# Scan stage of a two-layer decoder: late gate activations split in two, residual passes and two gate products moved

## The reference, cut to what matters

```python
xn = x * rsqrt(mean(x * x) + EPS) * norm_w
x_inner, z = split(xn @ in_proj_w.T, 2)          # 512 channels each
xc = silu(conv(x_inner) + conv_b)
x_ssm = xc @ x_proj_w.T                          # B (16), C (16), dt (1)
dt = softplus(x_ssm[..., -1:] * dt_w + dt_b)
A = -exp(A_log)
def step(h, inp):                                # over the 128 tokens
    dA = exp(dt_t[..., None] * A)
    h = dA * h + (dt_t * u_t)[..., None] * B_t[:, None, :]
    y_t = sum(h * C_t[:, None, :], axis=-1) + D_param * u_t
    return h, y_t
y = scan(step) * silu(z)
out = y @ out_proj_w.T + residual
```

## Time and profile before

| what | value |
|---|---|
| runs | 852.97, 853.94, 859.43 us |
| median | 853.94 us |
| profiled execution: its own time | 856.85 us |
| its span in the trace | 854.6 us |
| mean granted TensorE clock (share of full speed) | 0.923 |
| PE busy | 694.7 us (81%) |
| DVE busy | 673.3 us (79%) |
| ACT busy | 529.8 us (62%) |
| POOL busy | 497.3 us (58%) |
| first scan starts, last scan starts | 575.9, 732.3 us |

### The profile page before, as it was taken

One profiled execution on the slowest core, in us unless ns is written; L12 is line 12 of the kernel. 1 busy time (PEld: TensorE's weight loads), 2 busy tenths in 40 slices (PEclk: granted clock), 3 DMA queues, 4 the chain that ended last, 5 costly groups with the idle time before them and its releaser, 6 DMA issues. The chain is left out here.

```text
span 854.6 us, 22547 instructions
## 1 busy us (share of the span) xinstructions
PE 694.7 (81%) x8285; PEld 522.1 (61%) x8285; DVE 673.3 (79%) x1498; ACT 529.8 (62%) x1439; POOL 497.3 (58%) x528
## 2 busy tenths in 40 slices
PE   4899999999999989369999708988889988851464
PEld 3578888888888776158899503345555555441333
DVE  6767778898888976667788557789889998679867
ACT  2644555566555655236676595579899787019296
POOL 2057777777777875045555176118899898424211
PEclk9999999999999999669999858999999999975778
DMA  7827000000000410027775533032333332010001
GB/s 295 279 94 301 1 2 2 7 1 8 1 8 8 161 51 14 7 69 217 225 201 147 120 115 89 2 100 78 102 101 127 103 108 96 3 49 0 1 13 38
DMA packets 30347, 71.44 MB, mean 84 GB/s; under 512 B 5472, under 2 KB 19488, under 8 KB 28320
## 3 DMA queue, kind: packets, MB, share of 16 engines
q1 hardware_dynamic: 25680, 57.54, 19.3%
q0 software_dynamic: 4560, 12.46, 6.1%
HBM read 59.57 MB, written 10.42 MB: 82 GB/s over the span
## 5 line engine op out<-in xcount | busy, mean ns | idle before, releaser
L1911 POOL TENSOR_TENSOR arena<-arena 128x1024 f32<-128x1024 f32 x63 | 147.2, 2385 | 29.1 <-DVE arena L1850 23.5
L1850 DVE TENSOR_TENSOR_SCAN arena<-arena,ps 128x1024 f32<-128x1024 f32 x64 | 141.8, 2270 | 14.1 <-ACT arena L1720 6.9
L1537 PEld LDWEIGHTS ps<-arena 64*64 64x64 f32 x4096 | 79.6, 134 | 63.9 <-DVE arena L1850 25.5
L1537 PE MATMUL ps<-arena 64*64 64x64 f32 x4096 | 92.0, 223 | 17.9 <-issue 8.9
L647 PE MATMUL ps<-arena 128*128 128x128 f32 (+1 forms) x768 | 101.2, 282 | 0.9 <-PEq L376 0.9
L647 PEld LDWEIGHTS ps<-arena 128*128 128x128 f32 (+1 forms) x768 | 91.7, 193 | 14.1 <-issue 12.9
L852 ACT ACTIVATE arena<-arena 128x128 f32<-128x128 f32 x256 | 98.8, 390 | 1.2 <-DVE arena L776 1.1
L1088 POOL DMA_INDIRECT arena<-tokens,arena x63 | 60.8, 965 | 59.6 <-PE ps L1124 42.4
L860 ACT ACTIVATE arena<-ps 128x512 f32<-128x512 f32 x64 | 38.2, 597 | 86.6 <-PE ps L666 86.6
L907 POOL TENSOR_TENSOR arena<-arena 128x512 f32<-128x512 f32 x64 | 66.7, 1043 | 21.5 <-DVE arena L782 21.5
L897 POOL TENSOR_TENSOR arena<-arena 128x256 f32<-128x256 f32 x64 | 47.9, 748 | 46.2 <-DVE arena L762 46.2
(11 more groups left out here) (326 smaller groups left out, 1522.1 us busy)
## 6 DMA issues: line engine op xcount, KB each, us to landing
arena<-c_rows SPq DMA_DIRECT2D x32, 512.0 KB, 3.7
arena<-in_E_gu SPq DMA_DIRECT2D x8, 1024.0 KB, 12.9
expert_out<-arena SPq DMA_DIRECT2D x63, 128.0 KB
arena<-in_E_dn SPq DMA_DIRECT2D x1, 4096.0 KB, 13.3
arena<-in_ctxT SPq DMA_DIRECT2D x2, 1024.0 KB, 5.1
arena<-in_A_o SPq DMA_DIRECT2D x1, 2048.0 KB, 16.6
arena<-in_X_o SPq DMA_DIRECT2D x1, 2048.0 KB, 23.7
arena<-in_F_w SPq DMA_DIRECT2D x4, 512.0 KB, 5.2
```

The source lines that it names most:

```text
L1537: t = eng.matmul(psD[d][cols, k, at:at + R], dtuT[rows, b, c, cols], diagB[rows, i % 2, b, :], start=True, stop=True)
L1850: eng.tensor_tensor_scan(hst[s % 4], dA[s % 4], psD[s % 2].rearrange("p k m -> p (k m)"), 0.0, ALU.mult, ALU.add).then_inc(h_ready, 1)
L1911: eng.tensor_tensor(hC[s % 4], hst[s % 4], Csb[i % 4], ALU.mult).then_inc(hC_ready, 1)
```

## The change

In ScalarE's loop the residual passes move from i = 2 to 9 to i = 17 to 24. The two Silus of i = 10 go; in their place come one Silu at i = 14 (tiles 0 and 1, second token half, 1024 elements), and one behind the loop, after the last decay (tiles 2 and 3, both halves, 2048 elements). The gates of tiles 0 and 1 now wait for the first of these alone, and those of tiles 2 and 3 for both. On VectorE gate(0) and gate(1) move from behind scan 34 to behind scan 35. Nothing else differs.

```diff
                     decay(2 * i + 1)
-                    if i == 2:
+                    if i == ST - 2:
+                        eng.wait_ge(z_moved, Z_MOVED)
+                        eng.wait_ge(z_copied, Z_COPIED)
+                        eng.activation(zs[:, 0:Z_FIRST, HT:], zs[:, 0:Z_FIRST, HT:], ACT.Silu).then_inc(zs_ready, 1)
                         eng.wait_ge(normS.h_ready, NB)
                         eng.wait_ge(res_step, 5)
-                    if i - 2 < NB:
-                        residual(i - 2)
-                    if i == ST // 2 + 2:
-                        eng.wait_ge(z_moved, Z_MOVED)
-                        eng.wait_ge(z_copied, Z_COPIED)
-                        eng.activation(zs[:, Z_FIRST:, 0:HT], zs[:, Z_FIRST:, 0:HT], ACT.Silu).then_inc(zs_ready, 1)
-                        eng.activation(zs[:, :, HT:], zs[:, :, HT:], ACT.Silu).then_inc(zs_ready, 1)
+                    if ST < i <= ST + NB:
+                        residual(i - ST - 1)
+                eng.activation(zs[:, Z_FIRST:], zs[:, Z_FIRST:], ACT.Silu).then_inc(zs_ready, 1)
 ...
                 def gate(c):
                     k = c % 2
                     eng.wait_ge(y_done, 2 * ST * (c // 2) + (2 * ST if c < 2 else 2 * ST - 1 + k))
-                    eng.wait_ge(zs_ready, 2)
+                    eng.wait_ge(zs_ready, 1 + c // 2)
 ...
                     scan(s)
-                    if s == 2 * ST + 2:
+                    if s == 2 * ST + 3:
                         gate(0)
                         gate(1)
```

## The result

Over 20 runs of each, the changed kernel took 860.02 us (median), the kernel before 855.75 us: a ratio of 1.0051, 95% interval 1.0034 to 1.0068, so 0.5% or 4.4 us slower. The forecast was no change (853.6 us on a median of 853.94, range 851.6 to 856.0). The profiled execution after took 863.45 us, the longest of its 20, with a span of 861.7 us (854.6 before, 7.1 less).

A forecast was written before the change was run, and what follows sets the result against it. GpSimd's products plus its pauses were taken to bound the scan stage. The terms -1.91 + 0.5 + 1.15 + 0 = -0.26 us, rounded to -0.3, on a median of 853.94 gave 853.6 us, range 851.6 to 856.0.

The forecast's parts named there:

- The gain of 1.91 us at turn 10: Scan stage, slots 22 and 23: without the early Silu block GpSimd's pauses of 1.34 and 0.57 us go; gain 1.91 us.
- a rival on the side of a gain: TensorE's instruction pauses shrink when it comes later, so the gates cost nothing and -1.91 us stays; 852.0 us, chance 0.23.
- The stall at turn 14 and the lag: New Silu block stalls VectorE 1.5 us (1.1 to 1.75), below GpSimd's delay behind the scans, some 2.4 us; no GpSimd pause.
- The loss of lag at slot 34: At slot 34 GpSimd's delay behind the scan falls from 1.9 to 1.45 us, so scan 34 ends 0.5 us later; cost 0.5.
- The gates one scan later: Gates behind scan 35 end 1.3 us later, delaying slot 36's product through TensorE; cost 1.15 us, bounds 0 to 1.3.
- Residual passes in the second half: Eight ScalarE passes, 3.9 us, moved to turns 17 to 24, hide in its waits for dBu; cost 0.
- The last Silu, and the load in the next block: Silu after the last decay hidden by 10 us; extra 1.28 us table load fits a 1.39 us cover; cost 0 to 0.1.
- The rival of a tail behind each table switch: Each table switch holds ScalarE for another load's length beyond its row; +3.6 us, 857.5 us, chance 0.03.
- The rival with the slower end: At slot 30 GpSimd's delay is shorter than the turn 14 stall, so GpSimd pauses; +1.7 us, 855.6 us, chance 0.18.

The follow-up runs named there:

- the split alone: Kernel before with only the Silus split (one at turn 14, one behind the last decay); 1.0017 of the kernel before.
- small loads: Kernel before, and changed kernel, with loads of C's rows cut from 1024 to 16 elements a partition from i = 4 on; 0.9933 and 0.9969 of kernel before.
- dummy block: Changed kernel with the two Silus of turn 10 put back, their results overwritten later; 1.0097 of the kernel before.
- the second pair of profiles: Kernel before and changed kernel, unaltered, each profiled once more; scan stage 158.2 and 160.1 us.
- C in halves: Kernel before, and changed kernel, with each row of C loaded as two 256 KB halves, the second one product later; 1.0057 and 1.0039 of kernel before.

## Why the prediction was wrong

- **The gain of 1.91 us at turn 10.** Half right, and the step that failed. The two pauses of GpSimd went. What I did not ask is what TensorE would do once nothing stalled it there. I had its pauses in my rows, 8.9 us, and took them as fixed; I used them only for a rival on the side of a gain. They depend on how TensorE's fetches fall between the loads of C, and the stall at turn 10 shifted that. In place of a gain slots 14 to 34 lost 2.6 us, 1.9 for the split alone. What the prediction counted as a stall of 1.91 us that can be won back was, in the five profiles that had it, also what kept 3.8 to 4.8 us of other pauses away.
- **The stall at turn 14 and the lag.** Forecast 1.1 to 1.75 us of stall, 1.5 taken; 1.8 (small loads) to 2.05 us (dummy block) measured where no pause hides it. The loss of lag at slot 34 was 1.2 us in place of 0.5 with small loads. Too small a term, of the right sign. The lag that the stall met was also guessed too large: 2.0 us at slot 29 with small loads, where the prediction took 2.4 at slot 30. Its own figures give 1.8 - 0.42 + 10 x 0.14 = 2.8 there, so the 2.4 was no result of them.
- **The gates one scan later.** The mechanism and the chain were right: no wait ahead of them, an idle VectorE ahead of scan 37, +1.05 us with small loads and +1.0 alone, against 1.15. In the changed kernel it was 2.1, which is the second term that failed. Missing was that TensorE, standing still behind the gates' wait for 2.84 us, would drop to half its clock and take 1.3 us more for y(32, 0). I named what is queued behind the wait, and not what the wait does to the engine that waits. GpSimd's pause was 5.19 us, not 4.
- **Residual passes in the second half: 0.** Right; 62.5 us from slot 38 to the end with them late, and 62.5 before.
- **The last Silu, and the load in the next block: 0 to 0.1.** Right; the cover was 1.39 us and the load 1.28. The rival of a tail behind each table switch fell: load and Silu follow each other at 647.29, 648.59, 649.66 with 1.28 us a load. The 1283 ns of the Trainium skill (ScalarE: Activation LUTs, What ACT_TABLE_LOAD costs) agree with the rows; no row shows the draining that it adds.
- **The rival with the slower end** (lag too short) had the right sign, +1.7 us, and its condition came true: late fetches held VectorE back, and the lag was 1.0 us at slot 29. But it let them cost only what the stall by ScalarE at slot 30 then passed on to GpSimd; in the rows they cost directly, in GpSimd's pauses for TensorE at slots 26 to 30, which begin four slots ahead of that stall. Its sum, 855.6, was still 4.4 us under the result.
- **The base.** Of the 6.4 us between the forecast of 853.6 and the measured 860.02, 1.8 are the kernel before itself: its median over 20 runs is 855.75, and over the three that the forecast started from it was 853.94.
- Against the pair of profiles the loss in the stage is accounted for: -0.3 (slot 0 to 14) + 2.6 + 2.1 + 0.1 = 4.5 us. That this is also the 4.4 us of the 20 runs is partly chance: the early pauses alone move an execution by 3.4 us, the second pair of profiles differs by 1.8 us in the stage, and both pairs differ by a further 2.6 and 4.0 us outside it.

## What to carry to other kernels

An engine that runs long straight-line code has a hidden input, its instructions, and here they travelled on the same 16 DMA engines as the data: pauses that the trace calls "issue" in the middle of a run of equal instructions are to be set beside the DMA view before a stall elsewhere is taken as pure loss. Removing a stall that lies upstream of such an engine can move it into step with a periodic load and cost more than the stall did; an estimate should then reach at least as far as these pauses do. And before a wait is made longer, ask what the waiting engine does afterwards: TensorE came out of 2.84 us of waiting at half its clock here, though not in every kernel with such a wait.

## What the runs showed of the hardware

- With loads of 512 KB every two slots TensorE's pauses marked issue at its dBu matmuls (575 to 745 us) were 7.1 to 13.8 us; with loads of 8 KB they were 1.5 and 1.8. Loads of 256 KB, twice as often, gave 10.0 and 12.1.
- Every one of these pauses ends 2.1 to 3.0 us after the start of a 16 KB instruction packet on q8; 36 such packets come in the stage.
- Most pauses repeat from one execution of a kernel to the next to 0.5 us each, the worst to 0.8, but one group (slots 8 to 14, 3.4 us of time) can be wholly absent from an execution of the same kernel.
- In four profiles TensorE had waited 2.84, 2.30 (both the changed kernel), 3.04 (dummy block) and 1.65 us (changed kernel, C in halves) at the gates and ran on at a granted clock of 0.50; in two it had waited 1.92 and 3.04 us and stayed at 1.00. What tells them apart was not found.
